# A decoder layer on one core: the first-layer quantisation writes its bf16 tiles in 7 blocks of 64 with a stride of 65

## The reference

```python
x = x + attn(layernorm(x))                 # 16 heads of 32, rotary, causal
x = x + xattn(layernorm(x), ctx, ...)      # fp8-like quantised projections, see below
x = x + ffn(layernorm(x))                  # ternary weights, SiLU gate, RMS norm

def _div_clamp_fp8(x, scale):
    y = jnp.clip(x / scale, -448, 448)
    y = y.astype(bfloat16).astype(float32)
    return y.astype(float8_e4m3fn).astype(float32)
# in xattn: ln_out = _ln(hidden); q, k, v and qx each project
#   _div_clamp_fp8(ln_out, their own in_scale[512]) with their own weights
# and the output projection quantises the concatenated heads in the same way
```

## Time and profile before

| | |
|---|---|
| median of 3 runs | 1239.63 us (1236.75 to 1240.57) |
| the profiled execution | 1239.65 us, its span 1237.9 us |
| busy over the span: PE, PEld | 1171.4 us (95%), 783.1 us (63%) |
| DVE, ACT, POOL | 935.1 us (76%), 803.8 us (65%), 618.3 us (50%) |
| mean granted TensorE clock | 0.978 |
| the 32 calls of `l_q` | 95.6 to 256 us |

### The profile page before, as it was taken

How to read it: one execution, slowest core, us unless ns; L and a number is a source line. 1 busy time by engine, 2 the same in 40 slices (tenths; PEclk the granted TensorE clock), 3 DMA queues, 4 the chain that set the end, 5 groups by cost and what they waited for, 6 DMA issues and landing times.

```text
span 1237.9 us, 19189 instructions
## 1 busy us (share of the span) xinstructions
PE 1171.4 (95%) x6272; PEld 783.1 (63%) x6330; DVE 935.1 (76%) x2785; ACT 803.8 (65%) x2295; POOL 618.3 (50%) x769
## 2 busy tenths in 40 slices
PE   4999979889999999999999999999999999799998
PEld 2677767556666666676666766667666666455564
DVE  4669987999888887888999985657788777556242
ACT  4666558777877876676667765568776767663130
POOL 1547884654554455545566542215554455158172
PEclk9988999889999999999999999999999999899999
DMA  8210001212110221123332231022111110000000
GB/s 268 86 59 25 25 17 33 84 35 69 52 52 19 64 81 60 41 78 94 102 111 60 76 93 51 17 78 85 60 60 43 60 34 1 1 1 1 35 1 26
DMA packets 27476, 69.26 MB, mean 56 GB/s; under 512 B 2945, under 2 KB 9217, under 8 KB 27377
## 3 DMA queue, kind: packets, MB, share of 16 engines
q1 hardware_dynamic: 27104, 67.67, 17.4%
q10 hardware_dynamic: 272, 0.36, 0.1%
HBM read 61.21 MB, written 6.82 MB: 55 GB/s over the span
## 4 chain that ended last, share of the span: by engine, by line
PE 45%; DVE 28%; ACT 19%; POOL 4%; issue 2%; DMA 1%; ACTq 0%; POOLq 0%; SPq 0%
PE ps L870 10%; PE ps L1150 8%; PE ps L1081 7%; ACT big L799 6%; PE ps L860 4%; PE ps L1202 4%; DVE big L415 3%; PE ps L962 3%; PE ps L1029 3%; DVE big L982 3%; ACT big L965 2%; DVE big L243 2%; PE ps L994 2%; DVE big L662 2%; DVE big L663 2%
## 5 line engine op out<-in xcount | busy, mean ns | idle before, releaser
L870 PE MATMUL ps<-big 128*125 128x512 bf16 x1152 | 264.6, 379 | 0.0
L799 ACT ACTIVATE big<-ps,big 112x128 f32<-112x128 f32 (+1 forms) x512 | 192.4, 456 | 72.3 <-POOL big L433 69.5
L870 PEld LDWEIGHTS ps<-big 128*125 128x125 bf16 x1152 | 155.3, 136 | 79.9 <-ACT big L957 0.3
L860 PE MATMUL ps<-big 128*112 128x512 bf16 x768 | 190.4, 392 | 4.6 <-ACT big L957 2.0
L432 POOL TENSOR_TENSOR big<-big 112x4 f32<-112x4 f32 (+1 forms) x128 | 38.6, 301 | 310.4 <-ACT big L427 310.4
L666 POOL TENSOR_TENSOR big<-big 128x448 f32<-128x448 bf16 x96 | 102.8, 1071 | 104.8 <-DVE big L979 64.5
L860 PEld LDWEIGHTS ps<-big 128*112 128x112 bf16 x768 | 101.0, 134 | 70.3 <-issue 9.2
L982 DVE TENSOR_SCALAR big<-big 112x112 f32<-112x112 f32 (+1 forms) x256 | 133.8, 543 | 6.8
L965 ACT ACTIVATE big<-ps,big 112x375 f32<-112x375 f32 x128 | 74.7, 583 | 85.1 <-DVE big L964 84.0
L415 DVE BATCH_NORM_STATS2 big<-ps 112x6 f32<-112x128 f32 (+1 forms) x512 | 113.1, 282 | 18.8 <-PE ps L870 17.0
L1029 PE MATMUL ps<-big 125*128 125x224 f32 (+1 forms) x512 | 121.4, 360 | 5.5 <-DVE big L1011 4.8
(11 more groups left out here) (115 smaller groups left out, 2275.9 us busy)
## 6 DMA issues: line engine op xcount, KB each, us to landing
big<-in_ctx_t SPq DMA_DIRECT2D x32, 375.0 KB, 3.6
big<-in_w_s SPq DMA_DIRECT2D x16, 512.0 KB, 3.9
big<-in_w_p SPq DMA_DIRECT2D x16, 512.0 KB, 4.2
big<-in_w_x SPq DMA_DIRECT2D x16, 512.0 KB, 3.7
big<-in_w_g SPq DMA_DIRECT2D x16, 512.0 KB, 3.7
big<-in_w_d SPq DMA_DIRECT2D x8, 512.0 KB, 4.4
big<-in_w_a SPq DMA_DIRECT2D x8, 384.0 KB, 5.1
scr<-big SPq DMA_DIRECT2D x24, 128.0 KB, 1.7
```

The source lines that it names most:

```text
L799: t = act(lambda e, j=j: e.activation(z[0:rows, 128 * j:128 * j + 128], bk[0:rows, 128 * j:128 * j + 128], ACT.Identity, bias=rr[0:rows, 4 ...
L860: t = pe(lambda e, k=k, s=s, n=n: e.matmul(bk[0:T, :], xq[:, k, :], w[:, s, k, col:col + 512], start=n == 0, stop=n == 7), xq_tok[(v, b)], ...
L870: t = pe(lambda e, k=k, s=s, u=u, n=n: e.matmul(bk[0:CK, :], cT[:, s, k, CK * c:CK * c + CK], w[:, u, k, col:col + 512], start=n == 0, sto ...
```

## The change

Only `l_q` is touched: its 32 calls go to a new function `quant_blocks` in place of `quant`. It has the same six operations on the same engines in the same order. What differs is where the tiles lie. The dense bf16 tiles `y` and `m` now share the memory of the f32 tile `tt`, half each. The clamp reads dense `y` and writes `yb`, 7 blocks of 64 elements whose starts are 65 elements (130 bytes) apart. The mask reads `yb` and writes dense `m`. The floor reads dense `m` and writes `mb_`, again 7 blocks of 64 with a stride of 65. POOL's sum reads `yb` and `mb_`, and its difference reads `mb_`. So each of the three one-input DVE instructions has one side in a single row of 448 and the other in 7 rows of 64.

For this each bf16 tile of `chain` grows from 224 to 227 words. Two of the five `small2` tiles move to another area; all tiles allocated after them start 4 words (16 bytes) lower. `quant`, still used 64 times by `t_s4`, is the same but for the addresses: its `m` now starts 227 words after `y`, its `tt` 454.

```diff
-        chain = Ring([(b16(rings.take(224), 448), b16(rings.take(224), 448), f32(rings.take(448), 448))
+        chain = Ring([(b16(rings.take(227), 454), b16(rings.take(227), 454), f32(rings.take(448), 448))
                       for _ in range(2)])
         small = Ring([f32(rings.take(40), 40) for _ in range(5)])
-        small2 = Ring([f32(rings.take(8), 8) for _ in range(5)])
+        small2 = Ring([f32((consts if n < 2 else rings).take(8), 8) for n in range(5)])
...
         def quant(src, mul, dsts, toks):
 
             i, (y, m, tt), free = chain.take()
+            y, m = y[:, 0:448], m[:, 0:448]
...
+        def flat(v):
+            return v[:, 0:448].rearrange("p (a n) -> p a n", a=7)
+
+        def in_blocks(v):
+            return bass.AP(v.tensor, v.offset, [list(v.ap[0]), [65, 7], [1, 64]])
+
+        def quant_blocks(src, mul, dst, toks):
+
+            i, (yb, mb_, tt), free = chain.take()
+            y, m = tt[:, 0:224].bitcast(BF), tt[:, 224:448].bitcast(BF)
+            yb, mb_ = in_blocks(yb), in_blocks(mb_)
+            t1 = dve(lambda e: e.tensor_tensor(y.rearrange("p (k t) -> p k t", k=4), src, mul, ALU.mult), toks, free)
+            t2 = dve(lambda e: e.tensor_scalar(yb, flat(y), 448.0, -448.0, ALU.min, ALU.max), t1)
+            t2 = dve(lambda e: e.tensor_scalar(flat(m.bitcast(U16)), yb.bitcast(U16), 0x7FFF, None, ALU.bitwise_and), t2)
+            t3 = dve(lambda e: e.tensor_scalar(mb_, flat(m), P20, MFLOOR, ALU.mult, ALU.max), t2)
+            t4 = pool(lambda e: e.tensor_tensor(flat(tt), yb, mb_, ALU.add), t3)
+            t5 = pool(lambda e: e.tensor_tensor(dst, tt.rearrange("p (k t) -> p k t", k=4), mb_, ALU.subtract), t4)
+            chain.release(i, t5)
+            return t1, t5
...
         def l_q(it, vs, last):
...
-                t1, t5 = quant(f3, mul, [(dst, 0, T, None)], [tf, t_rsc])
+                t1, t5 = quant_blocks(f3, mul, dst, [tf, t_rsc])
```

## The result

The median is 1235.39 us (1231.84 to 1237.73, 15 runs) against 1238.60 us before (15 runs): a ratio of 0.9973, 95% interval 0.9965 to 0.9981. That is 3.2 us, where 8.7 were forecast. The profiled execution took 1234.79 us, its span 1233.0 us.

What follows compares the result with a forecast made beforehand. DVE was taken to bound to 183 us with PE close behind, PE to 207, DVE to 258, then PE. PE idle time 4.6 plus clock 5.1 less friction 1 gave 8.7 us: 1239.65 to 1231.0 us, range 1222 to 1241.

Steps and rivals of the forecast that it cites:

- The length: Each of the three one-input DVE instructions in the 32 calls would take 390 ns, 1.17 us a call.
- The lock: DVE's one-input instructions waiting out whole POOL instructions over a shared port pair; unequal rows would end this.
- The sum on DVE: The three one-input instructions, 95 to 191 us: 21.1 in place of 37.45 us, 16.4 us less.
- DVE's later part: From 191 to 258 us, 18.0 in place of 18.40 us: longer instructions eat what fewer locks give.
- B: Rival: PE takes all of the saving, the gap moves or the clock drops elsewhere; gain 0 to 3.7 us, chance 0.15.
- the shifted addresses I cost at nothing: New addresses of `chain`, `small2` and what follows: no cost, at most under 1 us on the 64 later calls.
- after 260 us ... that part moves with its start and gives nothing of its own: The PE-bound stretch after 260 us, PE busy 787.48 of 815 us, would only shift and gain nothing itself.
- what of it reaches the end: PE up to 183 us: 4.6 us of idle time recovered, plus 5.1 us from a clock drop not coming.
- mostly: The chain that ended last, in the first stretch, was said to run through DVE, mostly the changed instructions.
- POOL's rows of 64, 0.06 us longer each: POOL's sum and difference reading 7 rows: 2.4 us over 40 instructions, hidden by POOL's 13 us idle.
- friction of the two-input instructions, 1 us: Two-input DVE instructions meeting a POOL never held: 32 calls with some 0.03 us more, 1 us lost.

Runs made afterwards that it cites:

- the second profile: The changed kernel run once more, unaltered; median 1235.49 us, ratio 0.9973 to the kernel before.
- The allocation alone: The changed kernel's tile sizes and places, but the old `quant` in all 96 calls; median 1235.45 us, ratio 0.9964 to the kernel before.
- the joined rows: The changed kernel with the 7 blocks at stride 64 in place of 65, forming one row of 448; median 1234.86 us, ratio 0.9968 to the kernel before.
- the lightened PE: Third partial product of the first attention's projection left out, in the kernel before (1238.32 us) and in the changed kernel (1235.04 us).

## Why the prediction was wrong

**Right.** The length: 390 ns taken from L371 and L663, 386 to 392 measured. The lock: gone. The Trainium skill's rule for the mode ("Vector Engine (DVE) Microarchitecture Reference", "Performance modes"), that outer counts of 448 against 7 bar the two-port modes, agrees with the trace, by the stride of 64 that brings back 276 ns and waits of over 1 us. The sum on DVE, 16.4 us up to 191 us: the changed kernel's three lines have 6.98 + 7.03 + 6.95 = 20.96 us there, 16.5 less than in the earlier trace rows. DVE's later part: unchanged. For the blocks the rival that holds is B (the gap moves, the clock drops elsewhere), given 0.15; its 0 to 3.7 us take in the 3.2 measured, but these have a cause that B doesn't have.

**Wrong 1: "the shifted addresses I cost at nothing".** This was the whole gain. The sum on POOL went from 1.03 to 0.95 us in 96 calls, 64 of which I had thought untouched by the change. With it fell "after 260 us ... that part moves with its start and gives nothing of its own": the part behind the last of the 32 calls went from 982.7 to 979.1 us (979.4 in the second profile), about the whole gain of 3.2. The allocation alone gives 3.1 us, and with the old spacing 0.7 us is left by the ratio, within its interval nothing or 1.9. No row of before could price it, but it was an unknown cost and should have had a range with both signs.

**Wrong 2: "what of it reaches the end", 4.6 + 5.1 us.** The idle time of PE up to 183 us fell by 3.4 us (6.62 to 3.24), not 4.6, and the clock gave back nothing: 16.5 us at half before, 16.8 after. The gap ahead of the last L550 kept 2.29 us, among other things since the sum of POOL ahead of it, put at 1.03 us "without locks", took 1.79: it is DVE's two-input product that it meets there, and this was so before. Nor did the chain run "mostly" through the changed instructions: from 145 to 184 us they have 25% of it, POOL's sum and difference 20%. I had taken a drop behind one gap as that gap's price and let it vanish with the gap; it is a quantity that moved. The early stretch went from 86.9 to 86.5 us. What the unequal rows are worth shows in three kernels with one allocation: 1235.4 us with them, 1234.9 and 1235.5 without, no difference beyond the intervals.

**Wrong 3: POOL's rows of 64, 0.06 us longer each.** They cost nothing: the sum takes 957 ns in blocks and 955 in one row at the same spacing, and the difference L690 1005 in blocks and 1034 in one row (the kernel with stride 64).

**Near enough: friction of the two-input instructions, 1 us.** The 32 L685 add up to 21.7 us, the 32 L662 to 20.3, so 1.4 us more, through a few long ones (1558 ns at most against 894). On POOL such a meeting costs more, before as after: L666 up to 1.78 us, L689 up to 1.84. The Trainium skill says so ("SBUF — State Buffer", "Who interferes with whom"): a DVE instruction with two SBUF inputs contends with a POOL one that reads. The trace agrees: L689 took 1.79 us with L685 inside it. It is the part of the waiting that the change could not touch.

**Where the 15 us went.** Up to 181 us DVE has time to spare in the changed kernel: 7 us more cost about 1. 14 us less on POOL with 13 more on DVE changed nothing, and 58 matmuls fewer on PE changed nothing. Yet 12 us off DVE (with the shorter calls), or 19 off POOL, gave 6 us early. So no single engine's work holds the stretch, and the three engines and the clock hold it together. Before, DVE was full and hid PE's drops; after, DVE waits for PE, and PE runs at half speed where it did not before. This is argued from single profiles. The time at the low clock alone does not sort the kernels: of those with an early stretch of 86 to 89 us the joined rows have 10 us up to 207 us and the lightened PE 30 and 34, and the mask on ACT has 83.4 us with 17. What makes the clock fall at 128 us, with PE busy 4.00 of 4 us in both windows from 119 us on, stays open, and so does why the locked and the free kernel come out within half a us of each other.

## What to carry to other kernels

Taking 15 us off the fullest engine gave nothing in a stretch where a second and a third were within some 10% of it and the clock of the second changed its drops with every variant: before forecasting, ask what the next engine's time would be at the worst clock of that stretch, not at its best. A change of allocation is an edit to be priced: separate it with a kernel that has the new addresses and the old code before crediting the instructions. Mind also the part that the change is thought to leave alone: here the gain was there. And where a trick makes an instruction longer and frees it from waiting, try it only where it was waiting; with the first 16 of 32 calls that gave 1233.4 us, the least of the variants with the same work, but not beyond the intervals.

## What the runs showed of the hardware that was not expected

- POOL's sum of two bf16 rows of 448 took 1.033 us in the median with the inputs 224 words apart and 0.955 us at 227 words, over 96 calls each (least 1.024 and 0.949). Two f32 rows of 512 took 1.262 us at 512 and at 515 words alike.
- Rows of 64 at odd half-words cost neither DVE (386 to 392 ns, by the line through 277, 424 and 614 ns) nor POOL (0.957 against 0.955 us) anything.
- Leaving out 96 wide matmuls raised the time at the low clock from 95 to 207 us from 17 to 30 and 34 us and left the total as it was.
